# Graph network kernel: four product banks, a split normalization and a moved scaling in the stages around the sums

## What is computed

```python
h = maximum(layernorm(x), 0)
deg = segment_sum(ew, row); dinv = rsqrt(deg)
xw = h @ W
h7 = segment_sum(xw[col] * (dinv[row] * ew * dinv[col])[:, None], row) + b
x = x + relu(h7 @ W1 + b1) @ W2 + b2          # block 0
h = maximum(layernorm(x), 0)
y = h @ W_next                                 # product of block 1
norm = dinv1[row] * dinv1[col]                 # its sum follows
```

## Time and profile before

| | |
|---|---|
| median of three executions | 5644.59 us (5641.9 to 5658.6) |
| the profiled execution | 5645.52 us, span of its instructions 5643.8 us |
| mean granted TensorE clock | 0.894 |
| PE / DVE / ACT / POOL busy, share of the span | 76% / 68% / 29% / 60% |
| pair-loading stage | 173.3 us to the start of the next at 212.3 us |
| stage between the sums | 1108.2 us to about 1256 us |

### The profile page before, as it was taken

The page is one execution under the profiler, slowest core; times in us unless marked ns, Lnnn a source line. Parts: engine busy times, 40 slices in busy tenths (PEclk is TensorE's granted clock), DMA queues, the critical chain, the costliest instruction groups (busy, mean ns, idle before and its releaser), DMA issues. The chain is left out here.

```text
span 5643.8 us, 68840 instructions
## 1 busy us (share of the span) xinstructions
PE 4265.0 (76%) x19341; PEld 3356.3 (59%) x19341; DVE 3823.9 (68%) x8692; ACT 1617.9 (29%) x3857; POOL 3375.0 (60%) x3109
## 2 busy tenths in 40 slices
PE   4566666367777678887987888789788888878886
PEld 4455444254444566665885666678666667756665
DVE  6644444355555569998535999853599995679998
ACT  3333333230000332222343222234322223422221
POOL 2488888607777467774136777503677760067775
PEclk9788888689999889998998999899899998989898
DMA  4488888726666577776026777612677762067775
GB/s 156 99 123 122 121 120 122 124 76 195 208 209 204 169 235 239 239 242 195 19 77 211 240 238 239 190 41 77 191 240 242 235 197 71 15 207 237 230 240 165
DMA packets 508434, 959.75 MB, mean 170 GB/s; under 512 B 85845, under 2 KB 298019, under 8 KB 507250
## 3 DMA queue, kind: packets, MB, share of 16 engines
q0 software_dynamic: 224512, 549.90, 39.0%
q1 hardware_dynamic: 283426, 404.92, 22.4%
q10 hardware_dynamic: 128, 0.52, 0.0%
HBM read 718.56 MB, written 236.50 MB: 169 GB/s over the span
## 5 line engine op out<-in xcount | busy, mean ns | idle before, releaser
L1449 POOL DMA_INDIRECT L2a_rows<-kv_rows,typed_index x960 | 962.0, 1002 | 292.6 <-issue 292.6
L1754 PE MATMUL L2a_sums<-L2a_weighted,L2a_hot 128*128 128x264 f32 x2784 | 786.7, 428 | 207.4 <-DVE L2a_weighted L1604 174.1
L869 POOL DMA_INDIRECT sum_rows<-L0s_rows,L0s_row_of x464 | 736.7, 1588 | 153.9 <-issue 121.7
L1754 PEld LDWEIGHTS L2a_sums<-L2a_weighted,L2a_hot 128*128 128x128 f32 x2784 | 552.7, 208 | 351.2 <-DVE L2a_weighted L1604 200.5
L1743 PE MATMUL L2a_query<-x,L2a_turned 128*128 x2784 | 721.5, 406 | 48.2 <-ACT L2a_turned L1698 26.4
L1743 PEld LDWEIGHTS L2a_query<-x,L2a_turned 128*128 128x128 f32 x2784 | 563.1, 205 | 147.0 <-issue 54.0
L1274 POOL DMA_INDIRECT L1s_rows<-rows,index x464 | 456.6, 984 | 302.7 <-ACTq L87 161.6
L1449 POOL DMA_INDIRECT L3a_rows<-feature_rows,index x464 | 485.5, 1046 | 154.9 <-issue 154.9
L1004 PE MATMUL L0s_message<-features,L0s_share 128*128 x928 | 319.5, 504 | 293.2 <-ACT L0s_share L969 293.2
L1449 POOL DMA_INDIRECT hold<-kv_rows,typed_index x432 | 431.3, 998 | 173.6 <-issue 173.6
L2278 POOL TENSOR_SCALAR L2d_here<-hold,mask 128x256 f32<-128x256 f32 x200 | 186.7, 950 | 575.7 <-PE L2d_flips L2487 298.7
(11 more groups left out here) (418 smaller groups left out, 8409.1 us busy)
## 6 DMA issues: line engine op xcount, KB each, us to landing
code_rows<-L1s_code SPq DMA_DIRECT2D x116, 512.0 KB, 3.1
L3a_code<-code_rows SPq DMA_DIRECT2D x116, 512.0 KB, 4.0
L0s_wide<-source_rows SPq DMA_DIRECT2D x116, 256.0 KB, 4.0
L2a_turn<-turned_rows SPq DMA_DIRECT2D x87, 256.0 KB, 4.4
L2a_pens<-mask_rows SPq DMA_DIRECT2D x87, 256.0 KB
L2a_hot<-hot_rows SPq DMA_DIRECT2D x87, 256.0 KB, 3.8
kv_rows<-L2d_key_rows SPq DMA_DIRECT2D x50, 384.0 KB, 2.6
kv_rows<-L2d_value_rows SPq DMA_DIRECT2D x150, 128.0 KB, 2.4
```

What stands on the lines that cost most here:

```text
L869: pool.indirect_dma_start(c.sum_rows[u], bass.IndirectOffsetOnAxis(ap=row_of[:, 4 * n + u:4 * n + u + 1], axis=0), rows[n % ring][:, u, :] ...
L1449: pool.indirect_dma_start(rows[n % ring][:, u, :], None, table, bass.IndirectOffsetOnAxis(ap=index_of[:, t:t + 1], axis=0)).then_inc(lande ...
L1754: last = pe.matmul(sums[(m * WP + j) % held][:, :], hot[quad % 2][:, j % 2 * 2 + k, :], weighted[:, 2 * j + k, :], start=k == 0, stop=k == 1)
```

## The change

In `load_pairs` GpSimd's instruction is taken out; ScalarE scales `c.q` block by block, 25 instructions behind its four copies. In `between_sums` there are four product banks (`held`) for two; `mean`, `gap` and `shift` have two halves, used by even and odd groups; `root` keeps only the square root and is called at s = 2 for s = 1, as `shift_mean` is on VectorE; the five normalizations become a function `normalized`, called with the blocks (0, 1) at s = 3, (2, 3) at s = 4 and (4) at s = 0 of the next group, and for group 0 after UP 7, 8 and 9; `measure` waits only for the normalizations of two groups before.

```diff
@@ load_pairs
-        @block.gpsimd
-        def _(pool):
-            pool.tensor_tensor(c.q[:, :, :], c.q[:, :, :], spread(c.dinv[:, SRC, :], 2, D), ALU.mult)
...
             last.then_inc(split, 1)
+            for t in range(NB):
+                act.activation(c.q[:, t, :], c.q[:, t, :], ACT.Copy, scale=c.dinv[:, SRC, t:t + 1])
@@ between_sums
-    CN = NB // U
+    CN, held = NB // U, 4
     UP, NEXT = range(2)
+    LOTS = (0, 1), (2, 3), (4,)
...
-        mean, var, gap, shift = (st.sb(x, [P, U]) for x in ("mean", "var", "gap", "shift"))
+        mean, gap, shift = (st.sb(x, [P, 2, U]) for x in ("mean", "gap", "shift"))
+        var = st.sb("var", [P, U])
...
-        product = [st.ps(f"product{s}", [P, 512]) for s in range(2)]
+        product = [st.ps(f"product{s}", [P, 512]) for s in range(held)]
...
             def measure(g):
+                m, k = mean[:, g % 2, :], gap[:, g % 2, :]
                 dve.wait_ge(product_free, drawn[(UP, own(g).stop - 1)] + 1)
...
-                wait(dve, normed, g * U)
+                wait(dve, normed, (g - 1) * U)
...
-                if s == 1 and g + 1 < CN:
+                if s == 2 and g + 1 < CN:
                     shift_mean(g + 1)
...
             def root(g):
                 act.wait_ge(safe, g + 1)
-                act.activation(gap[:, :], var[:, :], ACT.Sqrt).then_inc(rooted, 1)
+                act.activation(gap[:, g % 2, :], var[:, :], ACT.Sqrt).then_inc(rooted, 1)
+
+            def normalized(g, blocks):
                 act.wait_ge(shifted, g + 1)
-                for k in range(U):
-                    act.activation(c.h[:, g * U + k, :], c.x[:, g * U + k, :], ACT.Relu, bias=shift[:, k:k + 1],
-                                   scale=gap[:, k:k + 1]).then_inc(normed, 1)
+                for k in blocks:
+                    act.activation(c.h[:, g * U + k, :], c.x[:, g * U + k, :], ACT.Relu, bias=shift[:, g % 2, k:k + 1],
+                                   scale=gap[:, g % 2, k:k + 1]).then_inc(normed, 1)
...
                     if t == U + 1:
                         root(0)
-                if kind == NEXT and t % U == 1 and t // U + 1 < CN:
-                    root(t // U + 1)
+                    if U + 2 <= t < 2 * U:
+                        normalized(0, LOTS[t - U - 2])
+                if kind == NEXT:
+                    g, s = t // U, t % U
+                    if s == 2 and g + 1 < CN:
+                        root(g + 1)
+                    if s >= 3 and g + 1 < CN:
+                        normalized(g + 1, LOTS[s - 3])
+                    if s == 0 and g >= 1:
+                        normalized(g, LOTS[2])
...
                     p = drawn[(NEXT, t)]
-                    wait(pe, product_free, p - 1)
+                    wait(pe, product_free, p - held + 1)
...
             def down(t):
                 p = drawn[(UP, t)]
                 pe.wait_ge(hidden_ready, t + 1)
-                wait(pe, product_free, p - 1)
+                wait(pe, product_free, p - held + 1)
```

More of the change, by code:

```diff
@@ L1104, in add_up @@
                 dve.wait_ge(product_ready, i + 1)
-                dve.tensor_tensor(part[:, t % 2, :], product[i % 2][:, 0:D], b2, ALU.add).then_inc(mid, 1)
+                dve.tensor_tensor(part[:, t % 2, :], product[i % held][:, 0:D], b2, ALU.add).then_inc(mid, 1)
                 dve.wait_ge(mid, t + 1)
@@ L1109, in measure @@
             def measure(g):
+                m, k = mean[:, g % 2, :], gap[:, g % 2, :]
                 dve.wait_ge(product_free, drawn[(UP, own(g).stop - 1)] + 1)
-                for k in range(U):
-                    last = dve.bn_stats(stats[:, k, :], c.x[:, g * U + k, :])
+                for s in range(U):
+                    last = dve.bn_stats(stats[:, s, :], c.x[:, g * U + s, :])
                 then(last)
-                wait(dve, normed, g * U)
[L1115 to L1118, removed]
+                wait(dve, normed, (g - 1) * U)
+                then(dve.tensor_tensor(m, stats[:, :, 1], stats[:, :, 4], ALU.add))
+                then(dve.tensor_tensor(k, stats[:, :, 1], stats[:, :, 4], ALU.subtract))
+                then(dve.tensor_scalar(m, m, -0.5, None, ALU.mult))
+                then(dve.tensor_tensor(k, k, k, ALU.mult))
                 then(dve.tensor_tensor(var[:, :], stats[:, :, 2], stats[:, :, 5], ALU.add))
                 then(dve.tensor_scalar(var[:, :], var[:, :], 1.0 / D, 1e-5, ALU.mult, ALU.add))
-                then(dve.scalar_tensor_tensor(var[:, :], gap[:, :], 0.25, var[:, :], ALU.mult, ALU.add))
+                then(dve.scalar_tensor_tensor(var[:, :], k, 0.25, var[:, :], ALU.mult, ALU.add))
                 dve.reciprocal(var[:, :], var[:, :]).then_inc(safe, 1)
@@ L1125, in shift_mean @@
                 dve.wait_ge(rooted, g + 1)
-                dve.tensor_tensor(shift[:, :], mean[:, :], gap[:, :], ALU.mult).then_inc(shifted, 1)
+                dve.tensor_tensor(shift[:, g % 2, :], mean[:, g % 2, :], gap[:, g % 2, :], ALU.mult).then_inc(shifted, 1)
             def scale_next(t):
@@ L1130, in scale_next @@
                 dve.wait_ge(product_ready, i + 1)
-                dve.tensor_scalar(c.q[:, t, 0:D], product[i % 2][:, 0:D], c.dinv[:, DST, t:t + 1], None, ALU.mult
+                dve.tensor_scalar(c.q[:, t, 0:D], product[i % held][:, 0:D], c.dinv[:, DST, t:t + 1], None, ALU.mult
                                   ).then_inc(product_free, 1)
@@ L1224, in work @@
                     p = drawn[(NEXT, t)]
-                    wait(pe, product_free, p - 1)
+                    wait(pe, product_free, p - held + 1)
                     for k in range(2):
-                        last = pe.matmul(product[p % 2][:, 0:D], turned[i % 3][:, k, :], w[:, k, :], start=k == 0,
+                        last = pe.matmul(product[p % held][:, 0:D], turned[i % 3][:, k, :], w[:, k, :], start=k == 0,
                                          stop=k == 1)
@@ L1233, in down @@
                 pe.wait_ge(hidden_ready, t + 1)
-                wait(pe, product_free, p - 1)
+                wait(pe, product_free, p - held + 1)
                 for j in range(2):
-                    last = pe.matmul(product[p % 2][:, 0:D], hidden[t % 2][:, j, :], w2[:, j, :], start=j == 0, stop=j == 1)
+                    last = pe.matmul(product[p % held][:, 0:D], hidden[t % 2][:, j, :], w2[:, j, :], start=j == 0, stop=j == 1)
                 last.then_inc(product_ready, 1)
```

## The result

| | before | after |
|---|---|---|
| median | 5646.35 us (5641.9 to 5658.6, 4 runs) | 5587.55 us (5586.21 to 5590.17, 4 runs) |
| profiled execution, span | 5645.52, 5643.8 us | 5590.17, 5588.5 us |
| mean granted clock | 0.894 | 0.901 |

A forecast was written before the change was run, and what follows sets the result against it. Bound: a VectorE mask-and-store chain in the pair stage; three TensorE waits and lost clock between the sums. Gains 5.45 + 1.1 + 6.4 + 6.8 + 7.9 + 2.2 = 29.9 us gave 5615 us, range 5600 to 5629.

The forecast's parts named there:

- Pair stage: Loading of pairs: without GpSimd's multiplication L519 falls to 0.64 us and the mask store goes out earlier; gain 5.45 us.
- First blocks: Up phase between the sums: four banks remove TensorE's wait for a bank, so the second table sum starts 1.1 us earlier.
- Periods: Between the sums, one table sum to the next: 21.5 us for 27.9 and 28.3, gains 6.4 and 6.8 us.
- clock term: TensorE falls to 1.2 GHz after each stall behind a table sum, so block N5 to N6 takes 5.77 us.
- rival 1: Between the sums, the clock stays high after the shorter stalls: 40.9 us saved, 5604 us; chance 0.20.
- To N15: Between the sums, last table sum to product block 15: 24.9 us for 32.8, gain 7.9; clock kept, 22.0.
- Tail: Between the sums, product block 15 to the end: 17.6 us for 19.8, gain 2.2; high clock 15.3, gain 4.5.
- rows 1 conflict: Pair stage: VectorE's L519 takes 6.09 us, held until GpSimd's multiplication L495 is done; the same operation elsewhere takes 0.64.
- wait (a): Between the sums: VectorE's five summing instructions (add_tables, 7.8 us) hold a TensorE flip, 3.15 us idle; expected to remain.
- Rival 2: Mask store lands no earlier and normalization lots of two don't fit TensorE's gaps: 17.4 us saved, 5627; chance 0.16 with halves.
- rival 3: Between the sums, short waits from lots and bank order keep TensorE at 1.2 GHz: 21 us slower, 5666 us; chance 0.04.
- Rival 4: Between the sums, table stalls hide the rest of the edit: only 9.8 us saved in all, 5635 us; chance 0.05.

The follow-up runs named there:

- e5: The kernel before with four product banks alone; 5648.38 us, where before beside it took 5647.07.
- e6: The changed kernel with the pair-loading edit undone and two product banks for four, leaving the normalization edit; 5639.91 us (before beside it 5647.07).
- e9: The changed kernel with a GpSimd memset of 8 columns added in the pair stage; 5590.51 us, ratio 0.9891 to before.
- e12: The changed kernel with VectorE's marks L903 as four tensor_scalar instead of one tensor_tensor; ratio 0.9946 to before.
- f3: The changed kernel with a GpSimd multiplication in the pair stage whose result nothing uses; 5620.34 us (before beside it 5653.37).

## Why the prediction fell short

The direction was right, the size was not: 59 us for 30, outside the range. By its own steps:

- **Pair stage: right**, 5.4 for 5.45 us. L519's counterpart 0.64, the store at 194.31 where 192.5 was written (the stage began 1.7 us later). ScalarE's copies took 10.06 us, 0.40 each, less than both bounds (12.9 and 14.1); they are hidden, so it changes nothing. The Trainium skill's "ScalarE: Activation LUTs", section "What ACT_TABLE_LOAD costs", gives a cost for each pointer operand and an overlap between neighbours; an estimate from its figures for one pointer at 256 columns is 0.40 us, and the row agrees.
- **First blocks: under-sized**, 2.4 for 1.1 us. T2 comes at +35.86 us for +38.22. Banks alone give 0.9 (e5), the normalization 0.1 (e6), both 1.1 to 2.7 over the traces. It was reckoned from one wait of rows 4; what comes on top appears only with both edits, and was not traced further.
- **Periods: the steps right, the clock term mis-sized.** Flip at +6.5, N5 at +6.75 (6.85), pairs of 3.06 around the lots, last product to the sum 2.74 (2.73). What failed is the choice "so I take 1.2 GHz. From N5 to N6 then 5.77 us" at every restart. Behind T2 it was not paid at all: 18.63 us, the 18.6 of rival 1. Behind T3 it was paid in part: N5 to N6 4.72, period 20.33 for 21.5. To N15: 23.70, between 24.9 and 22.0. The cold case exists (e9: 21.3 us); a fixed price for it does not.
- **Tail: the clock again**, 14.83 us; 15.3 was the high-clock end, 17.6 taken. Together the stage gave 9.2 us over forecast. About 4 are the clock's luck in this execution: e9 and e12, the coldest, still gained 29.5, 5 over forecast: T2 2.4 us sooner for 1.1, T3 to T4 20.3 for 21.5, the rest behind T4.
- **Source sums: missed**, 13.1 us, the largest single miss. The failing sentence is the first: "which part of the program the change touches, because only there can time come from". It put the stages without an edit at nothing; with these 13.1 us added back the measured median would be 5601, at the edge of the range. The pair edit takes away GpSimd's multiplication ahead of 464 GpSimd issues. Its price has two terms: 7 ns on each issue (3.2 us), and fewer issues held by VectorE, L903 above all (9.0 us; how the multiplication brings it about stays open). The rows 1 conflict was in hand; the same pair of engines was not looked for anywhere else.
- **A reading**: wait (a) is called "five summing instructions"; add_tables is four on 128x1280 and five on 128x256, 7.9 us together, so the sum stands.
- **Left over:** about 3 us over the rest of the program, within what stages vary by.

Rival 1 was right for T2 to T3 and the tail. Rival 2 is refuted (pairs of 3.06 around the lots, the store lands earlier), as is rival 3: with four banks used in turn the clock was 1.00 from 1157.5 to 1166. So what the Trainium skill tells of one kernel in "TensorE: Matmul & The Clock Gate", section "A second HAM failure mode: psum-queue depth-cycling", does not show in this trace. Rival 4 is refuted by e6, 20 us from the normalization alone.

## What to carry to other kernels

In these traces GpSimd's instructions and indirect DMA issues waited for what was left of a VectorE instruction on SBUF data, of one input as of two, and L519 waited for GpSimd: look for every such pair in the program before costing a move of GpSimd work, fear the long instructions most, and compare the shortest, median and longest duration of a row rather than its mean. A bound that sorts out the worst cases can hide that milder ones have the same cause. When a stall nears 3 us, carry both clock levels into the sum as separate cases, and prefer an edit that cuts the stall, as the two-part table sums did. Edits that remove consecutive waits on one engine are to be costed together: four banks alone gave 5.8 us, behind the split normalization 9.5 or more.

## What the runs showed of the hardware

- GpSimd's indirect DMA issues last 1545 ns, but 1552 for the whole next stage once GpSimd has multiplied in the stage ahead; a memset does not do it. Seen in 17 of 17 traces (1551 to 1553 against 1545 or 1546), without a known cause.
- VectorE's tensor_tensor of 0.69 us holds such an issue for what is left of it less about 0.12 us. Its tensor_scalar of 0.35 us does the same, by 0.14 us at most, so that four of them for the tensor_tensor leave one long issue or none where there were 32.
- A GpSimd tensor_scalar was held by VectorE's tensor_scalar with one SBUF input (1.30 us for 0.92 with 0.50 us left), not by a memset or a copy from PSUM (0.91 and 0.92).
- GpSimd's tensor_scalar in pieces of 0.92 us lets VectorE in between two of them (L520 0.64 us); one instruction of 11.29 us held L519 for its whole rest (6.09 us).
- TensorE behind an idle time of 3.46 us ran on at 2.4 GHz in five traces and at 1.2 GHz in four; behind 3.15 us it fell in an execution (after) in which it had kept 2.4 GHz behind 3.46, and kept it in one (f3) in which it had fallen behind 3.46.
